# Sums of squares of keys and queries in a linear-attention mixer: from many two-column matmuls to streamed squares

## What is computed

```python
for i in range(DEPTH):                                   # 2 layers
    y = layernorm(x, ln1_g[i], ln1_b[i])
    q = (y @ Wq[i] + bq[i]).reshape(B, N, HEADS, DIM_HEAD).transpose(0, 2, 1, 3)   # 8 heads of 64
    k = (y @ Wk[i] + bk[i]).reshape(B, N, HEADS, DIM_HEAD).transpose(0, 2, 1, 3)
    v = (y @ Wv[i] + bv[i]).reshape(B, N, HEADS, DIM_HEAD).transpose(0, 2, 1, 3)
    qp = softmax_kernel(q, proj[i], True)
    kp = softmax_kernel(k, proj[i], False)
...
def softmax_kernel(data, proj, is_query, eps=0.0001):
    normalizer = d ** (-0.25)
    data_dash = jnp.einsum('bhnd,md->bhnm', data * normalizer, proj)
    diag = jnp.sum(data ** 2, axis=-1, keepdims=True) * 0.5 * normalizer ** 2
    m = max of data_dash over the last axis (queries), or over the last two (keys)
    return ratio * (jnp.exp(data_dash - diag - m) + eps)
```

## Time and profile before

| | |
|---|---|
| median of 3 runs | 2229.84 us (2223.46 to 2231.34) |
| the profiled execution, own time | 2227.69 us |
| its span, first to last instruction | 2225.9 us |
| mean granted TensorE clock | 0.931 |
| PE busy | 1960.4 us, 88%, 9764 matmuls |
| DVE, ACT, POOL busy | 891.4 (40%), 607.0 (27%), 592.4 us (27%) |
| DMA | 160.62 MB, 72 GB/s on average |

### The profile page before, as it was taken

One profiled execution on the slowest core, in us unless ns is written; L12 is line 12 of the kernel. 1 busy time (PEld: TensorE's weight loads), 2 busy tenths in 40 slices (PEclk: granted clock), 3 DMA queues, 4 the chain that ended last, 5 costly groups with the idle time before them and its releaser, 6 DMA issues. The chain is left out here.

```text
span 2225.9 us, 28867 instructions
## 1 busy us (share of the span) xinstructions
PE 1960.4 (88%) x9764; PEld 1607.9 (72%) x9765; DVE 891.4 (40%) x1745; ACT 607.0 (27%) x1113; POOL 592.4 (27%) x408
## 2 busy tenths in 40 slices
PE   0767998999999989998989989999799898899992
PEld 0444656888888867776979977788688798778881
DVE  8777612111111134444134446422532353462237
ACT  5722102111111111104234552112142364331110
POOL 3000213232323123206312003433262300063332
PEclk9999898999999999998787899999888798999996
DMA  2010402121311285226621100111164111001111
GB/s 52 1 48 0 153 0 81 72 104 71 104 71 66 94 284 165 95 86 164 169 73 40 46 20 1 39 38 39 55 166 131 47 43 62 1 29 48 39 47 46
DMA packets 75221, 160.62 MB, mean 72 GB/s; under 512 B 9616, under 2 KB 24500, under 8 KB 73306
## 3 DMA queue, kind: packets, MB, share of 16 engines
q1 hardware_dynamic: 75092, 158.92, 22.3%
HBM read 103.30 MB, written 55.59 MB: 71 GB/s over the span
## 5 line engine op out<-in xcount | busy, mean ns | idle before, releaser
L561 PE MATMUL ps<-yT,wslot 128*128 128x500 f32 (+1 forms) x576 | 210.3, 365 | 13.4 <-POOL wslot L1706 4.8
L563 PE MATMUL ps<-yT,wslot 128*128 128x500 f32 (+1 forms) x576 | 206.8, 359 | 0.0
L562 PE MATMUL ps<-yT,wslot 128*128 128x500 f32 (+1 forms) x576 | 206.8, 359 | 0.0
L787 PE MATMUL ps<-g,adj 125*125 125x512 f32 x800 | 191.3, 402 | 16.9 <-issue 16.9
L787 PEld LDWEIGHTS ps<-g,adj 125*125 125x125 f32 x800 | 151.4, 190 | 56.8 <-issue 18.2
L1706 POOL TENSOR_TENSOR wslot<-mix_landing,wslot 128x2048 fp32r<-128x2048 f32 x24 | 110.9, 4622 | 213.3 <-ACT wslot L1389 213.3
L1710 POOL TENSOR_TENSOR hidT<-qpT,hidT 128x500 fp32r<-128x500 f32 (+1 forms) x96 | 104.4, 1090 | 197.9 <-DVE hidT L1544 197.9
L358 PE MATMUL ps<-key_hot,row_hot 125*125 125x500 bf16 x430 | 106.4, 388 | 46.0 <-DVE key_hot L328 35.8
L561 PE MATMUL ps<-parts,w 128*128 128x500 f32 (+1 forms) x384 | 136.4, 355 | 6.2 <-DVE bl L904 6.2
L1440 ACT ACTIVATE qpT<-ps,layer_cols 128x500 f32<-128x500 f32 (+1 forms) x96 | 58.2, 609 | 287.7 <-PE ps L563 243.0
L562 PE MATMUL ps<-parts,w 128*128 128x500 f32 (+1 forms) x384 | 136.3, 355 | 0.0
(11 more groups left out here) (262 smaller groups left out, 3822.4 us busy)
## 6 DMA issues: line engine op xcount, KB each, us to landing
mix_landing<-in_L_mix_W SPq DMA_DIRECT2D x16, 1024.0 KB, 5.1
qk_dram<-qk_parts SPq DMA_DIRECT2D x128, 125.0 KB, 2.4
g_dram<-staged SPq DMA_DIRECT2D x40, 256.0 KB, 2.0
u_dram<-staged SPq DMA_DIRECT2D x40, 256.0 KB, 2.0
g_in<-g_dram SPq DMA_DIRECT2D x40, 256.0 KB, 3.6
u_in<-u_dram SPq DMA_DIRECT2D x40, 256.0 KB, 2.7
k_stack<-qk_dram SPq DMA_DIRECT2D x8, 1250.0 KB, 6.2
q_stack<-qk_dram SPq DMA_DIRECT2D x8, 1250.0 KB, 8.2
```

The source lines that it names most:

```text
L561: nc.tensor.matmul(out, lhs_high, rhs_high, start=first, stop=False)
L562: nc.tensor.matmul(out, lhs_high, rhs_low, start=False, stop=False)
L563: return nc.tensor.matmul(out, lhs_low, rhs_high, start=False, stop=last)
L787: last = nc.tensor.matmul(m.ps[0:P, t % 2, :], counts if exact else counts.bitcast(F32), part if exact else part.bitcast(F32), start=(s == ...
```

## The change

The squares no longer stay in SBUF as whole rows, held by PE tile by tile. They become the streamed operand: for each piece ACT writes the square twice, in full (`square`, two slots) and rounded to `F32R` (`square_parts`, part 0, a ring of four), and DVE subtracts the second from the first to part 1. Two pieces later PE holds an `F32R` matrix `halves[:, g, :]` of 16 columns (columns 2g and 2g + 1 are the halves of the pair's two heads, the others zero) and streams both parts past it, 500 or 250 columns. All pieces of one chunk, both sides, add up in one bank (3, 2 or 1), 16 partitions by the chunk's columns. ACT copies these three to SBUF (`keep_diagonals`), and ten transposes of 16 x 125 turn them back, into bank 5, behind the third value tile; DVE copies them to `diag` behind the fourth. To free the banks, the transposes of the third row group share banks 0 and 1, and the value tiles alternate between banks 0 and 4.

```diff
-        diag = sb("diag", [P, 2, PAIRS, T, 2])
+        diag = sb("diag", [P, T, 2, PAIRS, 2])
...
-                def diagonals(i, side):
-
-                    pe.wait_ge(qk_copied, i * 2 * NQ + (side + 1) * NQ)
-                    for j in range(PAIRS):
-                        for t in range(T):
-                            at = ((SIDES[side][1] * PAIRS + j) * T + t) * 2
-                            last = nc.tensor.matmul(m.ps[0:P, 2, at:at + 2], squares[side][j][:, tile(t)], halves[:], start=True, stop=True)
+                def diagonal(i, n):
+
+                    side, (c, f) = n // NQ, divmod(n % NQ, K)
+                    cn = CHUNKS[c][1]
+                    pe.wait_ge(square_low, i * 2 * NQ + n + 1)
+                    for part in range(2):
+                        last = nc.tensor.matmul(m.ps[0:4 * PAIRS, DIAG_BANK[c], 0:cn], halves[:, SIDES[side][1] * PAIRS + f, :],
+                                                square_parts[:, n % SQ_RING, part, 0:cn], start=(side == 0 and f == 0 and part == 0),
+                                                stop=(side == 1 and f == K - 1 and part == 1))
+                    last.then_inc(diag_summed, 1)
+
+                def turn_diagonals(i):
+
+                    for t in range(T):
+                        at = t % 4 * P
+                        last = nc.tensor.transpose(m.ps[0:P, 5, t * 4 * PAIRS:(t + 1) * 4 * PAIRS], diag_rows(t // 4)[:, at:at + P],
+                                                   m.ident[0:4 * PAIRS, 0:4 * PAIRS])
                     last.then_inc(diag_summed, 1)
...
                                 last.then_inc(qk_summed, 1)
+                                if n == SQ_LAG:
+                                    pe.wait_ge(eps_ready, 2)
+                                if n >= SQ_LAG:
+                                    diagonal(i, n - SQ_LAG)
                                 n += 1
                             if side == 0 and c == 0:
                                 turn_rows(i, 0, 2)
-                            if side == 1 and c == 0:
-                                pe.wait_ge(halves_ready, 1)
-                                diagonals(i, 0)
...
                     for t in range(T):
+                        if t == 2:
+                            pe.wait_ge(diag_copied, i * DIAG_COPIES + len(CHUNKS))
...
-                        if t == 1:
-                            diagonals(i, 1)
-                            pe.wait_ge(qk_copied, i * 2 * NQ + 2 * NQ)
+                        if t == 0:
+                            for n in range(2 * NQ - SQ_LAG, 2 * NQ):
+                                diagonal(i, n)
+                        if t == 2:
+                            turn_diagonals(i)
...
-                            nc.scalar.activation(squares[side][f][:, c0:c0 + cn], m.ps[:, 4 + n % 4, 0:cn], ACT.Square,
+                            if n >= 2:
+                                act.wait_ge(square_low, i * 2 * NQ + n - 1)
+                            nc.scalar.activation(square[:, n % 2, 0:cn], m.ps[:, 4 + n % 4, 0:cn], ACT.Square,
+                                                 bias=qk_bias[:, a, f:f + 1], scale=NORM)
+                            if n >= SQ_RING:
+                                act.wait_ge(diag_summed, i * DIAG_STEPS + n - SQ_RING + 1)
+                            nc.scalar.activation(square_parts[:, n % SQ_RING, 0, 0:cn], m.ps[:, 4 + n % 4, 0:cn], ACT.Square,
                                                  bias=qk_bias[:, a, f:f + 1], scale=NORM).then_inc(qk_copied, 1)
+
+                    def keep_diagonals(c):
+
+                        act.wait_ge(diag_summed, i * DIAG_STEPS + NQ + (c + 1) * K)
+                        nc.scalar.activation(diag_rows(c)[:, 0:CHUNKS[c][1]], m.ps[0:4 * PAIRS, DIAG_BANK[c], 0:CHUNKS[c][1]], ACT.Copy)\
+                            .then_inc(diag_copied, 1)
...
                     for c in range(len(CHUNKS)):
                         project(1, c)
+                        if c:
+                            keep_diagonals(c - 1)
+                    keep_diagonals(2)
...
                             nc.vector.tensor_copy(qk_parts[:, f, 0, 0:cn], qk_tmp[:, n % 2, 0:cn]).then_inc(qk_high, 1)
+                            vec.wait_ge(qk_copied, i * 2 * NQ + (n + 1))
+                            nc.vector.tensor_tensor(square_parts[:, n % SQ_RING, 1, 0:cn], square[:, n % 2, 0:cn],
+                                                    square_parts[:, n % SQ_RING, 0, 0:cn].bitcast(F32), ALU.subtract).then_inc(square_low, 1)
...
                         if t == 0:
+                            vec.wait_ge(diag_summed, i * DIAG_STEPS + 2 * NQ)
                             nc.vector.memset(v[:, :, :, DH:VW], 1.0)
...
-                        if t == 2:
-                            vec.wait_ge(diag_summed, i * 2 + 2)
-                            nc.vector.tensor_copy(diag[:].rearrange("p a j t h -> p (a j t h)"), m.ps[0:P, 2, 0:2 * PAIRS * T * 2]).then_inc(diag_copied, 1)
+                        if t == 3:
+                            vec.wait_ge(diag_summed, (i + 1) * DIAG_STEPS)
+                            nc.vector.tensor_copy(diag[:].rearrange("p t a j h -> p (t a j h)"), m.ps[0:P, 5, 0:2 * PAIRS * T * 2]).then_inc(diag_copied, 1)
```

More of the change, by code:

```diff
@@ L976, in stage_mixer @@
         projT = sb("projT", [128, 2, M], F32R)
-        halves = sb("halves", [128, 2])
         col_rows = m.col_rows
@@ L1031, in stage_mixer @@
         z = o
-        squares = [[place(f"squares{s}{n}", [128, N], F32, at + n * (T * D * 4 // PAIRS // 32 * 32)) for n in range(PAIRS)]
-                   for s, at in enumerate((at_v, at_o))]
-        assert T * D * 4 // PAIRS // 32 * 32 >= N * 4
+        SQ_RING, SQ_LAG = 4, 2
+        square = place("square", [128, 2, CHUNKS[0][1]], F32, at_v)
+        square_parts = place("square_parts", [128, SQ_RING, 2, CHUNKS[0][1]], F32R, at_v + 2 * CHUNKS[0][1] * 4)
+        halves = place("halves", [128, 2 * PAIRS, 4 * PAIRS], F32R, at_kp + 2 * KP_BYTES + D * 4)
+        assert (2 + 2 * SQ_RING) * CHUNKS[0][1] * 4 <= V_BYTES and at_kp + 2 * KP_BYTES + D * 4 + 8 * PAIRS * PAIRS * 4 <= nc.sbuf_top
         slots = [place(f"wslot{n}", [128, 2, K, D], F32R, (at_kp if n < 2 else at_v) + n % 2 * SLOT_BYTES) for n in range(4)]
@@ L1052, in stage_mixer @@
         diag_summed, eps_ready = sem("diag_summed"), sem("eps_ready")
-        diag_copied = sem("diag_copied")
+        diag_copied, square_low = sem("diag_copied"), sem("square_low")
         ks_summed, k_less_ready, k_top_ready, k_all_ready = sem("ks_summed"), sem("k_less_ready"), sem("k_top_ready"), sem("k_all_ready")
@@ L1094, in key_bank, with turn_home, diag_rows @@
             return 6 + t % 2 if j < EARLY else (2, 5)[t % 2]
+        DIAG_BANK, V_BANK = (3, 2, 1), (0, 4)
+        DIAG_STEPS = 2 * NQ + 1
+        DIAG_COPIES = len(CHUNKS) + 1
+        def turn_home(half, n, width):
+            if half or n < 2 * K:
+                return n % 4, slice(0, width)
+            return (n - 2 * K) // 2, slice((n - 2 * K) % 2 * width, ((n - 2 * K) % 2 + 1) * width)
+        def diag_rows(c):
+            return qpT[0:4 * PAIRS, c, :] if c < 2 else qp[0:4 * PAIRS, 0, :]
         CONTEXT_AT = [3, 5, 7, 9]
@@ L1178, in turn_rows @@
                             pe.wait_ge(exact_ready, i * SPLITS + (turn_split(half, n - 4) + 1))
+                        bank, to = turn_home(half, n, (t1 - t0) * P)
                         for t in range(t0, t1):
-                            last = nc.tensor.transpose(m.ps[:, n % 4, (t - t0) * P:(t - t0 + 1) * P], z[:, t, k * 128:(k + 1) * 128],
+                            last = nc.tensor.transpose(m.ps[:, bank, to][:, (t - t0) * P:(t - t0 + 1) * P], z[:, t, k * 128:(k + 1) * 128],
                                                        m.ident[0:P, 0:P])
@@ L1312, in _ @@
                         for k in range(K):
-                            last = emit_split_product(nc, m.ps[0:P, t % 2, :], [yT[:, h, k, tile(t)] for h in range(2)],
+                            last = emit_split_product(nc, m.ps[0:P, V_BANK[t % 2], :], [yT[:, h, k, tile(t)] for h in range(2)],
                                                       [wt[:, h, k, :] for h in range(2)], k == 0, k == K - 1)
                         last.then_inc(v_summed, 1)
-                        if t == 1:
-                            diagonals(i, 1)
-                            pe.wait_ge(qk_copied, i * 2 * NQ + 2 * NQ)
+                        if t == 0:
[3 more added lines that the diff above has]
+                            turn_diagonals(i)
                         for j, s in early_keys(t):
                             key_scores(i, j, s)
-                    pe.wait_ge(diag_copied, i + 1)
+                    pe.wait_ge(diag_copied, (i + 1) * DIAG_COPIES)
                     pe.wait_ge(v_ready, i * T + T)
@@ L1400, in scale_and_shift @@
                             n = g * K + k
```

(12 more changed lines are left out.)

9 lines of the change are left out of this document (4 added, 5 removed).

## The result

The changed kernel takes 2202.85 us (median of 4 runs, 2197.96 to 2203.66) against 2229.72 us: 26.9 us less, a ratio of 0.9882 with a 95% interval of 0.9859 to 0.9905. The forecast was 2196, 33.7 us less. An unaltered second set of runs of it, beside the first experiments, gave 2197.17 us against 2229.94 (0.9845, 0.9798 to 0.9892), 32.8 us less. So the two measurements put the gain at 27 and 33 us, and part of what follows is about why one differs from the next by as much as a fifth of the gain.

The account below looks back on a forecast made before the run. PE, busy 88% of the span, was taken to bound the kernel. 60.2 - 20.7 - 5.6 = 33.9 us off the profiled 2227.7 gives 2193.8; with 2.1 for the median of runs, forecast 2196 us, range 2184 to 2212.

Parts of the forecast that it names:

- Removed: 60.2 us: Four bursts of two-column matmuls on PE in the projections, 52.1 us, plus 8.1 us of low clock behind them, go.
- what follows is released by nothing but PE's own order: At the bursts: the work behind them waits for no other engine, so their full 52.1 us goes.
- less is gained: Rival: query pieces wait for stores the first burst hid, 2 to 5 us a layer; say 2208, chance 0.15.
- Added on PE: 20.7 us: Streamed squares of keys and queries, 9.1 us a layer, and ten small transposes, 1.2 us a layer.
- The float32 price: Slower rival: matmuls with 16 held columns cost 2.0 us per 500 columns; 144 us more, 2340, chance 0.03.
- the low clock behind the transposes: Possible slow value tile behind the ten transposes, 2.5 us a layer; left out of the sum.
- New waits: 5.6 us: PE waits at the two weight hand-overs, 2 x 1.2 and 2 x 0.8 us, plus 1.6 us low clock.
- The first hand-over: At the query weights: PE idle 3.6 us for late squares, of which 1.2 us a layer is new wait.
- The second: Hand-over of the value weights: PE waits 0.8 us a layer for the squares of piece 12.
- no query-side wait over a us: Sign that the forecast is right: among the query pieces PE waits no more than a microsecond.
- The pace of the other engines: In 500-column pieces ACT needs 2.0 us, DVE and POOL 2.4 us, PE 3.2 us, so PE sets the pace.
- behind the value tiles all loads and stores follow events on PE and move with it: After the projections: the later stages shift with PE; no cost was put on them.

Follow-up runs that it names:

- the other two profiles of kernels with bursts: The kernel before with two store DMAs a piece in place of four, 2227.36 us; the kernel before with POOL's bias additions moved earlier, 2217.81 us.
- the kernel with half the stores: The changed kernel with two store DMAs a piece in place of four (one per head, both parts in one): 2193.27 us, ratio 0.9851.

## Why the prediction was right, point by point

**Removed: 60.2 us.** Right as the price of the bursts: 60.9 when nothing else was late (56 to 57 against the other two profiles of kernels with bursts). The step "what follows is released by nothing but PE's own order" was true of the kernel before and misleading for one without the bursts, since 43.5 us is what came out with the stores as they were. The rival *less is gained* named this mechanism, with its place and its releaser, and put 2 to 5 us a layer on it. In the changed kernel it costs little (PE waits 1.07 us for it in layer one and not at all in layer two), since the streamed squares themselves slow the pieces down to nearly the pace of the stores.

**Added on PE: 20.7 us.** 0.23 us for 500 columns with 16 held, as taken; 1.19 us for ten transposes, as taken (1.2). Between the kernel with half the stores and the one with no bursts and half the stores the stretches differ by 13.0 and 13.9 us, 26.9 in all. The prediction had 20.7 + 5.6 = 26.3 for that. That is within the scatter of the stretches, so it bears the sum out and not each term. The float32 price, my rival on the slower side, is out. So is the low clock behind the transposes: the stage from 1103.00 to 1104.20 has the granted clock at full, and so have the products behind:

```profile
1103.00:1104.20 1.20, 1.20 (x11) 1.15 (x10) 0.69 (x1) 0.00 (x0) 0.27 (x1) 1.00 0.47 106
```

What the Trainium skill ("TensorE: Matmul & The Clock Gate", Part 4: PE-mode transpose) says of transposes and the clock does not show behind ten so short ones; for long runs of them this says nothing.

**New waits: 5.6 us.** The first hand-over, 3.6 us idle by the sum, measured 3.60 from start to start in both layers, released by DVE's subtraction. DVE shows the blocked copy and the subtraction behind it:

```profile
1052.24 4.27 DVE L1618 CAST qk_parts<-qk_tmp 128x250 fp32r<-128x250 f32 x1 [0.99 <-ACT qk_tmp L1459]
1056.43 0.41 DVE L1620 TENSOR_TENSOR square_parts<-square,square_parts 128x250 fp32r<-128x250 f32 x1
```

It is the row of before with a reader behind it. The second, 0.8 us a layer by the sum, was 2.1 us in layer one and none in layer two. That goes with the clock: I expected it low behind the idle in both layers, and in this execution it was low in layer two alone (0.50 of full speed from 1638.3 to 1641.8), so PE came later to the squares there and found them ready.

The sum came out near 5.6 because errors in its terms offset each other. Against the kernel before, the first idle is 0.9 us longer in each layer (3.60 from start to start for 2.66), for the 1.2 of the sum. In layer one 2.1 us of the second wait come to it, and 1.1 us near the end of the queries where DVE had waited for stores, which I had at nothing: "no query-side wait over a us" was wrong twice there. The 1.5 us of low clock that the kernel before had in that place fell away. In layer two the low clock cost 2.6 us (10.2 us from the late diagonal to the third one behind it, for 7.6 in layer one), where I had 1.6. Together that is some 6 us. The second profile of the changed kernel had the low clock behind the idle in both layers (0.57 and 0.50 over some 3 us), as I had expected, and its later waits for squares were smaller, 1.3 us in layer one and 0.4 in layer two. So wait and low clock took each other's place; no run sets the clock by itself.

**The pace of the other engines.** Right. The subtraction takes 0.67 us where it comes first and 1.27 behind POOL, and PE goes through the pieces without a step apart from the places above. In the first row DVE comes behind POOL's step (1049.44 to 1050.71); in the second it comes first, and POOL's step beside it takes 1.64 us for 1.27:

```profile
1049.97 1.27 DVE L1620 TENSOR_TENSOR square_parts<-square,square_parts 128x500 fp32r<-128x500 f32 x1 [0.61 <-ACT square_parts L1467]
...
1080.14 0.67 DVE L1620 TENSOR_TENSOR square_parts<-square,square_parts 128x500 fp32r<-128x500 f32 x1
```

**The sum.** 33.9 us by the account, 32.8 in the stretches of the first profile, 30.7 in the second, 26.9 and 32.8 in the medians. What I left out is the stage behind: "behind the value tiles all loads and stores follow events on PE and move with it" is true of the order and not of the phase. The row in which POOL blocks DVE for 2.13 us was in my hands. I used it for the pieces only, and not for the attention, where the same pair of engines meets in both kernels and the dear phase costs some 4 us a layer more than the cheap one. The forecast had 33.7 us of gain for the measured 26.9 and 32.8; how near it came in a given set of runs is in part luck.

What stays open: how DVE and POOL settle who goes first when POOL's additions follow each other without a pause. One DVE instruction got in after 0.27 us and another, in the same place of another execution, waited for all that were left; no run here tells them apart. That the low clock is what scatters the stretch of the kernel before between 145.8 and 150.5 us is read from the granted clock (mean 0.84 over the long one, 0.88 over the two short ones, with the same waits of PE), not tested.

## What to carry to other kernels

Price a removed block by what it gave the others time for, too: ask which queue was catching up under it (here SP's stores, 17 us for both layers), and test it by removing the block alone and with that queue relieved. When one operand's squares, sums or counts are wanted, stream the large side past a small held matrix: the price is the columns, 0.23 us for 500, and not a weight load for every 125. When a new consumer is put in order on the engine that bounds the kernel, look for the producer's worst row and not its median; and expect a second limit right behind the first: here lag and stores had to be changed together, since either alone gave nothing that can be told.

## What was not expected of the hardware

A DVE instruction with two SBUF inputs of 2 elements a row took 4.78 us amid POOL's ten additions of 1.23 us each: it ended with the last, so it was held for nearly four of them and not for one. The Trainium skill ("SBUF — State Buffer", Who interferes with whom) has the two excluding each other for one instruction; the trace agrees, and shows besides that the loser may lose several times over. Moving those additions was worth 8.9 us of 2226.7 in the kernel before, which is between a quarter and a third of what the whole change brought.
